# Attention in another order of tiles, with a block's sum and 128 columns of its first tile copied by ScalarE

## The reference, cut to what matters

```python
s = jnp.einsum('bthd,bshd->bhts', q, k) * scale
logits = DEG * jnp.log(jnp.abs(s) + 1e-30) + log_G[:, :, :, None] - log_G[:, :, None, :]
logits = jnp.where(mask, logits, -jnp.inf)
m = jax.lax.stop_gradient(jnp.max(logits, axis=-1, keepdims=True))
a = jnp.exp(logits - m)
a = jnp.where(mask, a, 0.0)
num = jnp.einsum('bhts,bshd->bthd', a, v)
den = jnp.sum(a, axis=-1).transpose(0, 2, 1)
y = num / (den[..., None] + 1e-06)
y = (y - mu) / jnp.sqrt(var + 1e-09) * ln_w
```

## Time and profile before

| what | us |
|---|---|
| median of 3 runs (lowest, highest) | 2027.95 (2026.43, 2030.56) |
| the profiled execution | 2029.22 |
| its span | 2027.2 |
| PE busy in the span | 1894.0 |
| DVE busy in the span | 1758.4 |
| ACT busy in the span | 1299.8 |
| POOL busy in the span | 822.6 |

### The profile page before, as it was taken

How to read it: one execution, slowest core, us unless ns; L and a number is a source line. 1 busy time by engine, 2 the same in 40 slices (tenths; PEclk the granted TensorE clock), 3 DMA queues, 4 the chain that set the end, 5 groups by cost and what they waited for, 6 DMA issues and landing times. The chain is left out here.

```text
span 2027.2 us, 37349 instructions
## 1 busy us (share of the span) xinstructions
PE 1894.0 (93%) x12827; PEld 1340.4 (66%) x12827; DVE 1758.4 (87%) x2762; ACT 1299.8 (64%) x2204; POOL 822.6 (41%) x687
## 2 busy tenths in 40 slices
PE   7999869999999999999999996899938999999997
PEld 6677635555555554545555553799838999999997
DVE  6999859999999999999999997777677788878774
ACT  4544458877788878788887873344435656566553
POOL 3777711222221222222122211466615566656653
PEclk9999979999999999999999997999957999999999
DMA  5887886667655577655576712344353343344342
GB/s 183 282 292 264 280 229 150 159 162 166 151 135 143 130 171 167 150 144 132 137 161 161 171 44 77 102 127 137 113 169 80 75 95 70 82 90 92 75 99 58
DMA packets 170055, 289.26 MB, mean 143 GB/s; under 512 B 52623, under 2 KB 126624, under 8 KB 163680
## 3 DMA queue, kind: packets, MB, share of 16 engines
q1 hardware_dynamic: 143344, 248.30, 45.9%
q0 software_dynamic: 15360, 20.99, 6.6%
q10 hardware_dynamic: 11184, 17.83, 2.8%
HBM read 159.84 MB, written 100.27 MB: 128 GB/s over the span
## 5 line engine op out<-in xcount | busy, mean ns | idle before, releaser
L1060 ACT ACTIVATE att_sb_a<-att_ps_s,att_sb_fg,att_sb_f 128x1024 f32<-128x1024 f32 x384 | 457.0, 1201 | 184.3 <-PE att_ps_s L1237 152.2
L1103 DVE TENSOR_TENSOR keep_sb_store<-keep_sb_store,att_sb_a 128x1024 f32<-128x1024 f32 (+2 forms) x528 | 526.4, 1024 | 14.0 <-ACT att_sb_a L1060 13.2
L1008 POOL TENSOR_SCALAR_AFFINE_SELECT att_sb_dec<-att_sb_dec 128x128 f32<-128x128 f32 x256 | 217.0, 850 | 757.8 <-ACT att_sb_dec L1050 757.8
L1258 PE MATMUL att_ps_off<-att_sb_a,att_sb_v 128*64 128x512 f32 x1488 | 355.3, 592 | 0.0
L1950 ACT ACTIVATE ffn_sb_h<-ffn_ps_p,ffn_sb_b_cols 128x256 f32<-128x256 f32 x320 | 151.9, 476 | 174.4 <-PE ffn_ps_p L2133 174.2
L1237 PEld LDWEIGHTS att_ps_s<-keep_sb_late,att_sb_k 64*128 64x128 f32 x1920 | 160.9, 185 | 116.8 <-issue 49.7
L1237 PE MATMUL att_ps_s<-keep_sb_late,att_sb_k 64*128 64x512 f32 (+3 forms) x1920 | 235.0, 375 | 1.6 <-DVE att_sb_a L1119 1.2
L1237 PEld LDWEIGHTS att_ps_s<-att_sb_q,att_sb_k 64*128 64x128 f32 x1824 | 152.9, 185 | 111.4 <-issue 46.3
L1237 PE MATMUL att_ps_s<-att_sb_q,att_sb_k 64*128 64x512 f32 (+3 forms) x1824 | 222.8, 374 | 1.4 <-DVE att_sb_a L1119 1.0
L2049 DVE TENSOR_TENSOR ffn_sb_h_lo<-ffn_sb_h,ffn_sb_h_hi 128x256 fp32r<-128x256 f32 x320 | 200.2, 671 | 21.0 <-ACT ffn_sb_h_hi L1943 19.7
L1119 DVE SCALAR_TENSOR_TENSOR att_sb_a<-att_ps_s,att_sb_dec 128x1024 f32<-128x1024 f32 (+3 forms) x256 | 208.2, 813 | 4.6 <-PE att_ps_s L1237 2.9
(11 more groups left out here) (260 smaller groups left out, 3488.9 us busy)
## 6 DMA issues: line engine op xcount, KB each, us to landing
q_rows<-early_sb_halves SPq DMA_DIRECT2D x32, 1024.0 KB, 5.0
att_sb_k<-k_rows SPq DMA_DIRECT2D x64, 512.0 KB, 16.5
att_sb_tops<-keep_sb_store SPq DMA_DIRECT2D x180, 128.0 KB, 2.4
close_sb_nT<-num_rows SPq DMA_DIRECT2D x34, 512.0 KB, 4.0
k_rows<-early_sb_halves SPq DMA_DIRECT2D x16, 1024.0 KB, 5.3
keep_sb_late<-q_rows SPq DMA_DIRECT2D x32, 512.0 KB, 14.4
num_rows<-att_sb_num SPq DMA_DIRECT2D x64, 256.0 KB, 3.2
keep_sb_raw<-L_ffn_W ACTq DMA_DIRECT2D x32, 512.0 KB, 3.8
```

The costliest lines, as they stand in the source:

```text
L1008: nc.gpsimd.affine_select(out=tile, in_=tile, compare_op=ALU.is_ge, fill=0.0, base=0, pattern=[[1, P]], channel_multiplier=-1).then_inc(de ...
L1060: nc.scalar.activation(x, s_ps[slot(op)][:, :, :], ACT.Square, scale=f[:, p, i - 1, s:s + 1], bias=fg[:, p, i - 1, s:s + 1]).then_inc(sq_d ...
L1103: nc.vector.tensor_tensor(x[:, :, c:TB], x[:, :, c:TB], y[:, :, c:TB], ALU.max).then_inc(max_done, 1)
L1258: last = nc.tensor.matmul(ps[h * HD:(h + 1) * HD, c:TB], v_tile, a[:, a_slot(op), h, c:TB], start=(s == 0), stop=(s == (ST * i if kind == ...
```

## The change

PATTERN becomes another order of the same 41 places, the numbers added to the places change for nearly all kinds of work, two pieces of work go from DVE to ACT, and one join takes two tiles at once.

- Block 0's sum: the copy of `own_ps` to `num` (512 numbers in each of 128 partitions, from PSUM) is made by ACT, in the new function `total` on ACT's list.
- Block 0's first tile: the copy of the whole first diag tile into `acc` goes. Its first 128 columns (both heads, 256 numbers a partition), which no later tile covers, are copied by ACT in the new function `corner`. The other 384 columns are joined with the second diag tile in one DVE instruction, which reads both tiles from their buffers.
- A new semaphore `corner` is waited for by SP before it moves block 0's maxima, by ACT and DVE before they write the buffer of that tile again, and by PE for the last pair's transposes.

```diff
-PATTERN = ("o1 d3 o1 d3 o1 d3 o1 d3 o2 o2 d1 o2 o2 d1 "
+PATTERN = ("o1 d3 o1 d3 d3 o1 d3 o1 o2 o2 d1 o2 d1 o2 "
...
-FOLDS = (0.50, 0.66, 0.68)
+FOLDS = (0.40, 0.50, 0.58)
...
         if op[1] == "off":
-            return place[op] + 3.32 if op[3] else place[op[:3] + (1,)] + 3.31
-        return place[op] + 5.7
+            return place[op] + 1.79 if op[3] else place[op[:3] + (1,)] + 1.78
+        if op[2:] == (0, 0):
+            return place[op[:3] + (1,)] + 2.82
+        return place[op] + 2.83
...
-    et_order = Order({(q, i): place[q, "off", i, 0] + 2.29 for q, i in blocks})
+    et_order = Order({(q, i): place[q, "off", i, 0] - 3.32 for q, i in blocks})
...
+    act_todo += [(place[q, "diag", 0, 0] + 5.25, "corner", (q,)) for q in range(PAIRS)]
+    act_todo += [(values_at(last_own(q, 0)) + 0.23, "total", (q, 0)) for q in range(PAIRS)]
     dve_todo = [(max_at(op), "max", op) for op in offs + diags]
-    dve_todo += [(place[op] + 1.54, "own", op) for op in diags]
+    dve_todo += [(place[op] - 0.2, "own", op) for op in diags]
...
+            def corner(q):
+
+                op = (q, "diag", 0, 0)
+                act.wait_ge(sq_done, sq_order.count(op))
+                if q:
+                    act.wait_ge(moved[0], 16 * ST * q)
+                nc.scalar.activation(acc[:, 0, :, 0:P], a[:, a_slot(op), :, 0:P], ACT.Copy).then_inc(corner_done, 1)
+
+            def total(q, i):
+                n = total_order.rank[q, i]
+                act.wait_ge(av_done, av_order.count(last_own(q, i)))
+                act.wait_ge(num_st[n % 2], n // 2 * 16)
+                nc.scalar.activation(num[:, n % 2, :], own_ps[:, :], ACT.Copy).then_inc(num_done, 1)
...
-                if kind == "diag" and s == 0 and i == 0:
-                    nc.vector.tensor_copy(x, y).then_inc(max_done, 1)
+                if kind == "diag" and s == 1 and i == 0:
+                    first_tile = a[:, a_slot((q, "diag", 0, 0)), :, :]
+                    nc.vector.tensor_tensor(x[:, :, c:TB], first_tile[:, :, c:TB], y[:, :, c:TB], ALU.max).then_inc(max_done, 2)
...
-                if i == 0:
-                    nc.vector.tensor_copy(num[:, n % 2, :], own_ps[:, :]).then_inc(num_done, 1)
```

More of the change, by code:

```diff
@@ L868, in attend @@
     pe_todo = [(place[op], "s", op) for op in place] + [(values_at(op), "av", op) for op in offs + diags]
[L869 to L872, removed]
+    act_todo = [(place[op] + (0 if op[1] == "off" else 1.98), "sq", op) for op in offs + diags]
+    act_todo += [(place[op] - 3.89, "dec", op) for op in diags]
+    act_todo += [(place[q, "off", i, 0] - 3.32, "et", (q, i)) for q, i in blocks]
+    act_todo += [(q * N + N * 0.72, "factors", (q + 1,)) for q in range(PAIRS - 1)]
+    act_todo += [(place[q, "diag", 0, 0] + 5.25, "corner", (q,)) for q in range(PAIRS)]
+    act_todo += [(values_at(last_own(q, 0)) + 0.23, "total", (q, 0)) for q in range(PAIRS)]
     dve_todo = [(max_at(op), "max", op) for op in offs + diags]
-    dve_todo += [(place[op] + 1.54, "own", op) for op in diags]
-    dve_todo += [(place[op] + 1.26, "row", op) for op in maxes]
+    dve_todo += [(place[op] - 0.2, "own", op) for op in diags]
+    dve_todo += [(place[op] - 0.18, "row", op) for op in maxes]
     dve_todo += [(max_at(last_off(q, i)) + 0.01, "scale", (q, i)) for q, i in blocks]
-    dve_todo += [(values_at(last_off(q, i)) + 1.17, "part", (q, i)) for q, i in blocks]
-    dve_todo += [(values_at(last_own(q, i)) + 0.42, "total", (q, i)) for q, i in owns]
+    dve_todo += [(values_at(last_off(q, i)) - 0.29, "part", (q, i)) for q, i in blocks]
+    dve_todo += [(values_at(last_own(q, i)) + 0.19, "total", (q, i)) for q, i in owns if i]
     dve_todo += [(fold_at(*op), "fold", op) for op in folds]
@@ L938, in attend @@
         moved = [m.sem(f"moved{i}") for i in range(NB)]
-        fold_done = m.sem("fold")
+        fold_done, corner_done = m.sem("fold"), m.sem("corner")
         prep_done, et_done, exp_done, dec_done = (m.sem(s) for s in ("prep", "et", "exp", "dec"))
@@ L948, in wait, with wait_corner @@
                 eng.wait_ge(sem, order.count(op))
+        def wait_corner(eng, op):
+            if op is not None and op[1:] == ("diag", 0, 0):
+                eng.wait_ge(corner_done, op[0] + 1)
         def arrived(eng, q):
@@ L983, in move @@
                 sp.wait_ge(max_done, max_order.count(last_own(q, i)))
+                if i == 0:
+                    sp.wait_ge(corner_done, q + 1)
                 if (q, i) == (0, 1):
@@ L1077, in _ @@
                     query_factor(*op)
+                elif what == "corner":
+                    corner(*op)
+                elif what == "total":
+                    total(*op)
                 else:
@@ L1086, in maximum @@
                 x, y, c = acc[:, i, :, :], a[:, a_slot(op), :, :], left(op)
-                if kind == "off" and s == 0:
+                if s == 0 and (kind == "off" or i == 0):
                     return
@@ L1091, in maximum @@
                 dve.wait_ge(sq_done, sq_order.count(op))
[L1092 removed]
+                if q and s == 1:
                     dve.wait_ge(moved[i], 16 * ST * q)
[L1094 to L1095 removed]
+                if kind == "diag" and s == 1 and i == 0:
+                    first_tile = a[:, a_slot((q, "diag", 0, 0)), :, :]
+                    nc.vector.tensor_tensor(x[:, :, c:TB], first_tile[:, :, c:TB], y[:, :, c:TB], ALU.max).then_inc(max_done, 2)
                 elif kind == "off" and s == 1:
@@ L1135, in total @@
                 dve.wait_ge(num_st[n % 2], n // 2 * 16)
-                if i == 0:
-                    nc.vector.tensor_copy(num[:, n % 2, :], own_ps[:, :]).then_inc(num_done, 1)
-                else:
-                    dve.wait_ge(part_done, part_order.count((q, i)))
-                    nc.vector.tensor_tensor(num[:, n % 2, :], part[:, et_order.rank[q, i] % 2, :], own_ps[:, :], ALU.add).then_inc(num_done, 1)
+                dve.wait_ge(part_done, part_order.count((q, i)))
+                nc.vector.tensor_tensor(num[:, n % 2, :], part[:, et_order.rank[q, i] % 2, :], own_ps[:, :], ALU.add).then_inc(num_done, 1)
             def fold(q, n):
```

21 lines of the change are left out of this document (12 added, 9 removed).

## The result

The kernel after takes 2031.82 us (median of 20 runs, 2028.99 to 2036.46), the kernel before in the same session 2029.23 (20 runs, 2026.40 to 2030.88): ratio 1.0014, interval [1.0008, 1.0021], or 2 to 4 us more. The forecast was 2022.3 us, with a range of 2014 to 2031.

The account below looks back on a forecast made before the run. The prediction took DVE to bound the body of 59.9 us, PE only 0.8 us below. Its terms, -19.2 + 7.3 + 7.2 - 1.0 = -5.7 us, led from 2027.95 to 2022.3 us, range 2014 to 2031.

Parts of the forecast that it names:

- Two copies, -19.2: On DVE, 16 each of the L1095 and L1137 copies at 0.60 us go away: 19.2 us less.
- The chained joins, +7.3: On DVE, 66 more joins or scalings directly follow a join of their own block, at 0.11 us each: 7.3 us more.
- The two are level, so the gain just fits, with nothing beyond it: In a body after the change, DVE needs 59.1 us and PE 59.0, so the forecast gain is just possible.
- My sum of starts for TensorE, 59.1: In a body before the change, PE's steps added from their starts fill 59.1 of 59.9 us.
- The start, +7.2: First pair: four squares move behind the second query factor's DMA wait, a loss of 6.6 to 7.7 us, taken as 7.2.
- ACT's new work, 0: On ACT, corner copy and sum, at most 1.1 us a body, fit into 12 us free: cost 0.
- The general shift, 0: Most new numbers move DVE's list by about -1.6 places: put at 0, 0.2 us gain to 0.3 loss a body allowed.
- The end, -1.0: In DVE's last chain the block 0 copy goes to ACT and PE waits less: 0 to 2 us gained, taken as 1.
- PE takes over and the start is not paid back: Rival: body stays 59.9 us and the start is lost, 2034 us; chance 0.18 together with ACT's sum stalling squares.
- The chains cost nothing: Rival: chained joins on DVE add no time, body 58.7, 2015 us; chance 0.12 together with a start that costs nothing.

Follow-up runs that it names:

- e3: The changed kernel's order and numbers, but both copies made by DVE as before; 1.0088 of the kernel before, body 60.53 us.
- e9: The kernel after with a chained join's two waits swapped, first for the previous join, then for the square; 1.0002 of the kernel before, body 59.51 us.
- e6: The kernel after with a pair's three folds on 512 of 1024 columns, 1.6 us a body less for VectorE; 0.9989 of the kernel before, body 59.40.
- e2: The kernel before in its old order, with only the two copies moved to ACT; 0.9982 of the kernel before, body 59.78 us.
- e5: The kernel before without the third score term in block 3's off tiles, so less work for TensorE; 0.9969 of the kernel before, body 59.75 us.
- e1: The kernel after with the first pair's query factors back at their old place; 0.9984 of the kernel before, body 59.70 us.
- e13: The kernel after with swapped join waits, first pair's factors at their old place and its second another 3.7 places later; 0.9923 of the kernel before, 2018.87 us.
- e15: The kernel before with only the first pair's second query factor later, at +6.0 instead of +2.29 in ScalarE's order; 0.9977 of the kernel before.
- e8: The kernel after with the diagonal tiles' squares back at +2.34 instead of +1.98 in ScalarE's order; 1.0046 of the kernel before, body 60.10 us.
- e4: The kernel after without the third score term in block 3's off tiles, so less work for TensorE; 0.9989 of the kernel before, body 59.45 us.
- e11: The kernel after with the first pair's query factors at their old place and the chained joins' waits swapped; 0.9979 of the kernel before, body 59.52 us.
- e10: The kernel after with the scaling's two waits swapped, the factor first, then the join; 1.0026 of the kernel before, body 59.88 us.

## Why the prediction was wrong

- **Two copies, -19.2: right.** No L1095 or L1137 copy is left. e3 puts their worth in this order at 13 us by the bodies, or at 15 by the ratios (1.0088 less 1.0014); the rest went into the waits around them (VectorE's other waits are 0.25 us a body in e3 and 0.64 after).
- **The chained joins, +7.3: mis-sized, the first step that failed.** The count was right, 4.2 more in a body against 66 / 16 = 4.1. The price was not: it was read from a scaling behind a join and applied to joins behind joins. Of the 53 before, 48 are such scalings, but the other 5 are joins, and the earlier trace rows held their price, 1.33 instead of 1.13. In the kernel after a join behind a join costs 0.19 to 0.20, and one in each body 0.28. The term measured 16 x 0.94 = 15.0 us.
- **"The two are level, so the gain just fits, with nothing beyond it": the second step that failed.** With the joins at the prediction's price of 0.11 the body is 59.51 (e9), not 59.1. My sum of starts for TensorE, 59.1, was made of undisturbed steps; with its waits for squares and products its floor is 59.40 (e6), and in the old order about 59.8 (e2). So the kernel before was held by both engines, VectorE at 59.75 (e5) and TensorE at about 59.8, under a body of 59.90. The sentence that TensorE stood 0.8 us below was wrong. How the missing 0.3 us is made up I did not settle; the records show TensorE waiting up to 0.8 us at a time for squares and products.
- **The start, +7.2: right in its mechanism, the number in part by luck.** The traces have 7.1 by the loads. But undoing the factors' move in e1 gave only 5.5, and the other 1.5 us stay with the factors back: they belong to the rest of the new order in the first pair, which I had put at nothing. e13 and e15 add what I had not seen: the wait cost the kernel before as well, and part of its cost is TensorE's clock at half behind it.
- **ACT's new work, 0: no cost seen.** The sum, estimated at 0.72 from the earlier trace rows, takes 0.60, and in the 13 bodies from 400 to 1180 us ScalarE never stands before it; only at the very end it waits 0.89. ScalarE's 22.7 us of waits for joins went, and 35.9 us of waits for VectorE's products came.
- **The general shift, 0: not separable, and not as harmless as I held it.** One of its parts, the place of the diagonal squares, is worth 0.41 us a body (e8).
- **The end, -1.0: right**, -1.2 from the last load on, 0.4 of which is the shorter body.
- **The rivals.** "PE takes over and the start is not paid back" was to give 2034 with a body of 59.9 and to decide from 59.5 on; with the measured 59.69 it gives 2034 - 0.21 x 15.5 = 2031, or +2.9 us, and the measured difference is +2.6. It is the case that happened, though not by TensorE alone: of the 0.59 us that the body missed, 0.17 go with the joins' waits (e9), 0.30 lie in TensorE's floor (e6), and the last 0.12 no run separates. "The chains cost nothing", after the Trainium skill's "VectorE: DVE Perf Modes", section "The DRAIN you can't avoid", is refuted by every chained step here, 0.11 us and more; the page measured copies, and no run here has a chain of copies. And the rule of the Trainium skill's "Perfetto Trace Analysis", section "Identifying the Most-Contended Engine", taken by weight loads alone (the page names the share of peak arithmetic beside them), would have TensorE half free, at 103 of 200 us. In e6 it holds the body at 59.40, with 1.6 us less for VectorE, so the traces disagree.

The sum again with what was measured: body 15.5 x -0.21 = -3.3, start +7.5 (7.1 with the shorter bodies in that stretch taken out), end -0.8: +3.4, against +3.2 in the attention and +2.6 between the medians.

## What to carry to other kernels

When two engines share a loop, the busy one is not the only one near its floor: a sum of undisturbed steps bounds the other from below only, and a cut of work on each engine alone, as in e4 and e6, shows the two floors. A price is to be read from the same pair of instructions that the change makes, not from a neighbour; a few such pairs at the edge of a loop are enough. And of what stands behind a wait for a transfer, move the wait, not the work: one factor 3.7 places later was worth 9.3 us at the start (e13 against e11), more than all the rest of the change.

## What was not expected of the hardware

- The same dependence between two VectorE instructions costs 0.11 to 0.13 us when the second carries the wait for the first itself, and 0.18 to 0.20 when the wait stands in an instruction of its own (e9 down, e10 up).
- A wait of ScalarE of 7.69 us at the start leaves TensorE idle, and its granted clock is at half for 10.2 us (e11, 284.5 to 294.7); with the wait at 3.55 us and work ahead of it the clock does not fall (e13).
- GpSimd's masks (L1008, L1018), the same 128x128 instruction throughout, differ in length from version to version: 863 ns before, 750 with the copies alone on ScalarE (e2), 749 with the order alone (e3), 653 after, and 578 in e6, where nothing but VectorE's folds differs from after. Spans on this engine are rough, and no run was made for the cause. Lines by form, 400 to 1180 us, before and after:

```profile
L1008 POOL TENSOR_SCALAR_AFFINE_SELECT att_sb_dec<-att_sb_dec 128x128 f32<-128x128 f32 x208 | 179.2, 863 | 599.1 <-ACT att_sb_dec L1050 599.1
```

```profile
L1018 POOL TENSOR_SCALAR_AFFINE_SELECT att_sb_dec<-att_sb_dec 128x128 f32<-128x128 f32 x210 | 137.2, 653 | 643.4 <-ACT att_sb_dec L1060 643.0
```
